# The causal mask of the last score block: added on VectorE in the maximum instead of on TensorE

## The chip, the core and the metric

The kernel runs on one core of a Trainium2 chip. The metric is the time of one execution on the device, in microseconds (us). The engines that matter here are PE (TensorE, matrix products), PEld (its weight loads), DVE (VectorE), ACT (ScalarE), POOL (GpSimd) and SP (it issues most transfers). They run side by side and wait for one another by semaphores. PE and DVE meet in PSUM: PE writes scores into a bank, DVE reads them out.

## What is computed

The program is a stack of four layers on a tensor of 4 x 512 x 256: an attention with rotary positions and biases, a mixture of experts with eight experts, a second attention, and a gated mixture of experts. Each is followed by a normalisation and added to its input. Only the two attentions are touched. Both have 16 heads of 16 numbers and a causal mask:

```python
scores = jnp.einsum('bshd,bthd->bhst', q, k) / jnp.sqrt(HEAD_DIM)
causal = jnp.tril(jnp.ones((S, S), dtype=bool))[None, None]
scores = jnp.where(causal, scores, -jnp.inf)
probs = jax.nn.softmax(scores, axis=-1)
out = jnp.einsum('bhst,bthd->bshd', probs, v)
```

The softmax needs the largest allowed score of every row, for every head and each of the 512 rows of a sequence.

## The kernel before

One function, `attention_phase`, is run twice: at about 31 to 235 us of the span for the first attention and at about 559 to 775 us for the second. Its work is cut into `STEPS` = 16 steps, one for each of 4 sequences and 4 groups of `HPG` = 4 heads. A step T has `MAXES` = 11 slots s. In slot s PE makes one **maxima unit** of step T (`max_unit`, L966): scores of 128 query rows against the keys that they may see. It then makes one **probability unit** of the step before (`prob_unit`, L985), which ACT turns into exponentials (L906) and POOL masks (L540). Fills of other work (projections, transposes, outputs) stand between them at fixed slots.

The maxima units of a step are, by `max_work`: k = 0 to 3, one head each, 512 keys wide; k = 4 to 7, 384 wide; k = 8 and 9, two heads each, 256 wide; and **k = 10, the four-head unit**: the first 128 rows of all four heads against their first 128 keys, four blocks of 128 columns in one PSUM bank. They rotate over `A_BANKS` = 3 banks (named `shared` in the first attention, `a_ps_a` in the second). PE waits on `a_free` before it takes a bank, DVE on `a_full` before it reads one.

DVE finds the maxima in `unit_max`. For k below 10 it uses a fused operation (L1274, L1280) that adds the mask `mask_f` to the scores, writes the sum to `masked_s`, and keeps the negated maximum, which a short second instruction (READ_ACCUMULATOR) puts into `nmax`. For k = 10 the mask is not added by DVE: PE adds it into the bank with one more product, the identity `identb` times `mask_q` in bfloat16 (L970), and one TENSOR_REDUCE (L1285) gives the four maxima.

After unit 10 DVE splits the maxima of the step into two parts (`split_max`, L1295 and L1297, tile `nm`). PE transposes `nm` in `less` (L996), which stands in slot 2 of the next step in the first attention and, in the second, between products with the values in slot 1. ACT copies the result next to the queries (L761), and only then can the probability units of that step start. PE does this work in its own fixed order, so where `nm` is late, everything behind L996 on PE is late. DVE too has a fixed order: between its maxima stand evacuations of projections (L1234, L1254), the division of outputs (L1305, L1307) and the normalisations.

The order of each engine is written out in the loops over T and s; nothing is scheduled at run time.

Of the kernel before, what the change touches and what calls it, by code (L numbers as in the profile page):

```python
# [13 lines left out]
ALU = mybir.AluOpType  # L14
ACT = mybir.ActivationFunctionType
AX_X = mybir.AxisListType.X

P = 128
BATCH, SEQ, D = 4, 512, 256
# [7 lines left out]
HPG = HEADS // GROUPS  # L27
STEPS = BATCH * GROUPS
EPS = 1e-5
NEG = -1e38  # L30
# [139 lines left out]
STACKS = 3  # L170
# [4 lines left out]
LEAD = 96  # L175
# [17 lines left out]
def max_work(k):  # L193

    if k < 4:
        return [(k, 3, 0)]
    if k < 8:
        return [(k - 4, 2, 0)]
    if k < 10:
        return [(2 * (k - 8), 1, 0), (2 * (k - 8) + 1, 1, 2 * P)]  # L200
    return [(h, 0, h * P) for h in range(HPG)]
# [95 lines left out]
def attention_phase(nc, keep, w, layer, route, w1=None, w2=None, early=None, stacks=None, wide=None, first=None):  # L297
# [15 lines left out]
    with ExitStack() as ctx:  # L313
# [639 lines left out]
        def _(pe):  # L953
            def max_unit(t, k):

                n = t * MAXES + k
                ps = ps_a[n % A_BANKS]
                need(pe, a_free, n - A_BANKS + 1)
                if n < HPG:
                    pe.wait_ge(first_keys[n], 16)  # L960
                work = max_work(k)
                i, wd = work[0][1], (work[0][1] + 1) * P
                together = min(len(work), PER_TILE)
                for n in range(0, len(work), together):
                    h, _, at = work[n]
                    last = nc.tensor.matmul(ps[:, at:at + together * wd], q_st[t % STACKS][0:LEAD, h // PER_TILE, i * P:wd],  # L966
                                            k_st[t % STACKS][0:LEAD, h:h + together, 0:wd], start=(n == 0), stop=(k < 10),
                                            skip_group_check=True)
                if k == 10:
                    last = nc.tensor.matmul(ps[:, :], identb[:, :], mask_q[:, :].unsqueeze(1).to_broadcast([P, HPG, P]),  # L970
                                            start=False, stop=True, skip_group_check=True)
                last.then_inc(a_full, 1)

            def prob_unit(t, k):
# [241 lines left out]
        def _(dve):  # L1216
# [48 lines left out]
            def unit_max(t, k):  # L1265
                n = t * MAXES + k
                ps = ps_a[n % A_BANKS]
                dve.wait_ge(a_full, n + 1)
                if k < 8:
                    i, h = 3 - k // 4, k % 4  # L1270
                    wd = (i + 1) * P
                    if n > 1:
                        dve.wait_ge(a_free, n - 1)
                    nc.vector.tensor_tensor_reduce(masked_s[n % 2][:, 0:wd], ps[:, 0:wd], mask_f[:, SEQ - wd:SEQ], -1.0,  # L1274
                                                   -NEG, ALU.add, ALU.min, nmax[:, t % 2, i, h:h + 1]).then_inc(a_free, 1)
                    return
                if k < 10:
                    dve.wait_ge(a_free, n - 1)
                    for h, i, at in max_work(k):
                        last = nc.vector.tensor_tensor_reduce(masked_s[n % 2][:, at:at + 2 * P], ps[:, at:at + 2 * P],  # L1280
                                                              mask_f[:, SEQ - 2 * P:SEQ], -1.0, -NEG, ALU.add, ALU.min,
                                                              nmax[:, t % 2, i, h:h + 1])
                    last.then_inc(a_free, 1)
                    return
                nc.vector.tensor_reduce(nmax[:, t % 2, 0, :], ps[:, :].rearrange("p (h n) -> p h n", h=HPG), AX_X, ALU.max,  # L1285
                                        negate=True).then_inc(a_free, 1)

            def split_max(t):

# [1366 lines left out]
```

## Time and profile before

| | us |
|---|---|
| median of 3 runs | 990.11 |
| lowest and highest | 988.4, 990.35 |
| the profiled execution | 992.42 |
| its span, first to last instruction | 990.7 |
| busy in the span: PE | 916.7 |
| PEld | 718.8 |
| DVE | 605.8 |
| ACT | 492.0 |
| POOL | 439.3 |

The profiled execution lies 1.7 us outside its span and 2.3 us above the median of the runs. PE is busy for 93% of the span. Its busy time counts matmuls from start to modelled end, and neighbours overlap, so what one more matmul costs is read from the distance of the ends, not from its duration. The same holds for DVE: the next operation often starts before the one before has ended.

### The profile page before, as it was taken

The page shows a single profiled execution, that of the slowest core. Times are in us where ns is not written, and L with a number is a line of the kernel's source. Part 1 is how long each engine was busy: PE and PEld are TensorE (multiplying, and loading weights), DVE is VectorE, ACT ScalarE, POOL GpSimd, SP SyncE. Part 2 cuts the span into 40 slices and gives each one's busy share as a digit, 9 for nine tenths or more (in the row PEclk, how much of TensorE's full clock was granted, in tenths as well). Part 3 has the DMA queues.
Part 4 walks back from the last instruction along what each step waited for, and adds up shares of the span by engine and source line. Part 5 has one row for each costly group of instructions (what it writes and reads, how often), then busy time and mean ns, then how long its engine had stood idle before and what let it go on. Part 6 is the DMA issues. An engine that isn't in the chain of part 4 may idle for free. (4 is left out here: it accounts for less than half of the span.)

```text
span 990.7 us, 16978 instructions
## 1 busy us (share of the span) xinstructions
PE 916.7 (93%) x5620; PEld 718.8 (73%) x5620; DVE 605.8 (61%) x1961; ACT 492.0 (50%) x887; POOL 439.3 (44%) x416
## 2 busy tenths in 40 slices
PE   6899999999899999999992889999999779999997
PEld 4566766765688999999982556576756468888886
DVE  5677798988763444444444687887786246363535
ACT  6366666665333344443336265767676344343332
POOL 4453444436742333232236455455263455535333
PEclk9799999999999999999995898999999699999999
DMA  5443222201225322323104663534320010212201
GB/s 186 159 177 112 97 75 97 75 20 41 102 99 190 136 86 96 138 103 130 69 21 139 222 223 96 177 113 159 123 75 23 1 54 1 97 45 74 81 39 42
DMA packets 51964, 98.88 MB, mean 100 GB/s; under 512 B 7579, under 2 KB 23835, under 8 KB 51766
## 3 DMA queue, kind: packets, MB, share of 16 engines
q1 hardware_dynamic: 48822, 89.62, 26.3%
q0 software_dynamic: 3072, 8.39, 2.7%
q8 instruction: 36, 0.59, 0.2%
q14 instruction: 34, 0.28, 0.1%
HBM read 61.63 MB, written 36.36 MB: 99 GB/s over the span
## 5 line engine op out<-in xcount | busy, mean ns | idle before, releaser
L906 ACT ACTIVATE a_probs<-a_ps_b 128x512 f32<-128x512 f32 x240 | 142.0, 602 | 65.3 <-PE a_ps_b L985 62.4
L540 POOL TENSOR_SCALAR_AFFINE_SELECT a_probs<-a_probs 128x512 f32<-128x512 f32 x128 | 80.8, 649 | 136.2 <-ACT a_probs L906 136.1
L2074 PE MATMUL exp_ps_o<-w_both,exp_h_hi 128*128 128x512 f32 x320 | 115.7, 402 | 0.7 <-POOL w_both L1960 0.7
L985 PE MATMUL a_ps_b<-a_q_st,a_k_st 104*128 104x256 f32 (+3 forms) x384 | 104.7, 335 | 2.9 <-ACT a_probs L906 2.1
L1987 ACT ACTIVATE exp_h_hi<-shared 128x320 fp32r<-128x320 f32 x128 | 54.3, 440 | 86.0 <-PE shared L2057 86.0
L1274 DVE CUSTOM_DVE_ANT_0 a_masked_s<-shared,a_mask_f 128x512 f32<-128x512 f32 (+1 forms) x128 | 76.6, 620 | 31.8 <-PE shared L966 29.5
L2220 POOL TENSOR_TENSOR dense_h_lo<-dense_mixed,dense_h_hi 128x512 fp32r<-128x512 f32 x40 | 53.2, 1330 | 96.6 <-ACT dense_h_hi L2285 96.6
L1274 DVE CUSTOM_DVE_ANT_0 a_masked_s<-a_ps_a,a_mask_f 128x512 f32<-128x512 f32 (+1 forms) x128 | 76.5, 621 | 31.6 <-PE a_ps_a L966 29.0
L966 PE MATMUL a_ps_a<-a_k_st,a_q_st 96*128 96x512 f32 (+1 forms) x192 | 89.7, 483 | 5.8 <-DVE a_nmax L1274 5.0
L2031 DVE SCALAR_TENSOR_TENSOR exp_h_lo<-shared,exp_h_hi 128x320 fp32r<-128x320 f32 x128 | 61.4, 490 | 54.6 <-ACT exp_h_hi L1987 53.8
L966 PE MATMUL shared<-a_k_st,a_q_st 96*128 96x512 f32 (+1 forms) x176 | 90.0, 519 | 3.1 <-DMA a_k_st<-scratch 3.1
L1006 PE MATMUL a_ps_pv<-a_probs,a_v 128*32 128x512 f32 (+3 forms) x1024 | 89.9, 461 | 3.2 <-POOL a_probs L540 3.2
L2076 PE MATMUL exp_ps_o<-w_both,exp_h_lo 128*128 128x256 f32 x320 | 89.7, 280 | 0.0
L985 PEld LDWEIGHTS a_ps_b<-a_q_st,a_k_st 104*128 104x128 f32 x384 | 71.8, 193 | 24.4 <-ACT a_probs L906 14.6
L2057 PE MATMUL shared<-exp_x_t_hi,w_hi 128*128 128x320 f32 x256 | 79.2, 309 | 0.3 <-DVEq L2024 0.3
L2057 PE MATMUL shared<-exp_x_t_hi,w_lo 128*128 128x320 f32 x256 | 79.1, 309 | 0.0
L2057 PE MATMUL shared<-exp_x_t_lo,w_hi 128*128 128x320 f32 x256 | 79.1, 309 | 0.0
L1960 POOL TENSOR_TENSOR w_both<-w_raw,w_both 128x2048 fp32r<-128x2048 f32 x8 | 37.1, 4640 | 86.6 <-ACT w_both L1977 86.6
L2074 PEld LDWEIGHTS exp_ps_o<-w_both,exp_h_hi 128*128 128x128 f32 x320 | 60.1, 188 | 13.9 <-issue 1.0
L906 ACT ACTIVATE a_probs<-shared 128x512 f32<-128x512 f32 x80 | 48.3, 604 | 43.2 <-PE shared L985 42.7
L2515 DVE TENSOR_TENSOR dense_product<-dense_gated,dense_ps_u 128x512 f32<-128x512 f32 x40 | 27.5, 687 | 66.9 <-PE dense_ps_u L2305 59.8
L2285 ACT CAST dense_h_hi<-dense_mixed 128x512 fp32r<-128x512 f32 x40 | 24.8, 620 | 81.7 <-DVE dense_mixed L2534 51.7
(326 smaller groups left out, 2244.8 us busy)
## 6 DMA issues: line engine op xcount, KB each, us to landing
w_raw<-in_m_w SPq DMA_DIRECT2D x16, 1024.0 KB, 5.4
scratch<-a_hi SPq DMA_DIRECT2D x24, 512.0 KB, 3.0
dense_mix_rows<-mix_rows SPq DMA_DIRECT2D x9, 768.0 KB, 6.4
scratch<-a_lo SPq DMA_DIRECT2D x24, 256.0 KB, 3.2
a_q_st<-scratch SPq DMA_DIRECT2D x64, 96.0 KB, 2.2
a_k_st<-scratch SPq DMA_DIRECT2D x64, 96.0 KB, 2.3
exp_rows<-dispatched SPq DMA_DIRECT2D x9, 640.0 KB, 3.9
dispatched<-kept_sub SPq DMA_DIRECT2D x9, 512.0 KB, 2.8
```

The source lines that it names most:

```text
L540: nc.gpsimd.affine_select(out=blocks, in_=blocks, compare_op=ALU.is_ge, fill=0.0, base=0, pattern=[[0, HPG], [1, P]], channel_multiplier=- ...
L906: nc.scalar.activation(probs[:, k, :], ps_b[k % B_BANKS][:, :], ACT.Exp, scale=scale).then_inc(exps, 1)
L966: last = nc.tensor.matmul(ps[:, at:at + together * wd], q_st[t % STACKS][0:LEAD, h // PER_TILE, i * P:wd], k_st[t % STACKS][0:LEAD, h:h + ...
L985: last = nc.tensor.matmul(ps[:, at:at + wd], k_st[t % STACKS][0:TAIL, h, j * P:(j + 1) * P], q_st[t % STACKS][0:TAIL, h // PER_TILE, j * P ...
L1006: last = nc.tensor.matmul(ps_pv[h * VW:(h + 1) * VW, at:SEQ], v[:, b % 2, j, g * HPG + h, :], rhs, start=(j == 0), stop=(j == 2), skip_gro ...
L1274: nc.vector.tensor_tensor_reduce(masked_s[n % 2][:, 0:wd], ps[:, 0:wd], mask_f[:, SEQ - wd:SEQ], -1.0, -NEG, ALU.add, ALU.min, nmax[:, t % ...
L1987: nc.scalar.activation(h[0][:, f, half * HALF:(half + 1) * HALF], ps_u[n % U_BANKS][:, 0:HALF], ACT.Relu).then_inc(u_hi, 1)
L2031: nc.vector.scalar_tensor_tensor(h[1][:, f, cols], ps_u[n % U_BANKS][:, 0:HALF], 0.0, h[0][:, f, cols].bitcast(F32), ALU.max, ALU.subtract ...
L2057: last = nc.tensor.matmul(ps_u[(2 * f + half) % U_BANKS][:, 0:HALF], (w1["hi"], w1["lo"])[i][:, c, f * P:(f + 1) * P], x_t[j][:, c * CAP + ...
L2074: nc.tensor.matmul(bank[:, :], h[0][:, f, rows_at], w2["both"][:, f, :, :].rearrange("p k d -> p (k d)"), start=(f == 0), stop=False, skip ...
L2076: last = nc.tensor.matmul(bank[:, 0:D], h[1][:, f, rows_at], w2["hi"][:, f, :], start=False, stop=(f == FC - 1), skip_group_check=True)
L2220: nc.gpsimd.tensor_tensor(h[1][:, (m - 1) % H_BUFS, :], mixed[(m - 1) % 2][:, :], h[0][:, (m - 1) % H_BUFS, :].bitcast(F32), ALU.subtract) ...
```

## The change

In both attentions PE no longer adds the mask to the four-head unit: L970 goes, and the score product's `stop` is now always true. DVE takes unit 10 as it takes the others: four fused operations of 128 columns, each with its READ_ACCUMULATOR, in place of one TENSOR_REDUCE over 512 columns. The last of the eight instructions releases the bank. Before them DVE also waits on `a_free` for the unit two before, since `masked_s` has two buffers.

```diff
--- before.py
+++ after.py
@@ -964,11 +964,8 @@
                 for n in range(0, len(work), together):
                     h, _, at = work[n]
                     last = nc.tensor.matmul(ps[:, at:at + together * wd], q_st[t % STACKS][0:LEAD, h // PER_TILE, i * P:wd],
-                                            k_st[t % STACKS][0:LEAD, h:h + together, 0:wd], start=(n == 0), stop=(k < 10),
+                                            k_st[t % STACKS][0:LEAD, h:h + together, 0:wd], start=(n == 0), stop=True,
                                             skip_group_check=True)
-                if k == 10:
-                    last = nc.tensor.matmul(ps[:, :], identb[:, :], mask_q[:, :].unsqueeze(1).to_broadcast([P, HPG, P]),
-                                            start=False, stop=True, skip_group_check=True)
                 last.then_inc(a_full, 1)
 
             def prob_unit(t, k):
@@ -1274,16 +1271,13 @@
                     nc.vector.tensor_tensor_reduce(masked_s[n % 2][:, 0:wd], ps[:, 0:wd], mask_f[:, SEQ - wd:SEQ], -1.0,
                                                    -NEG, ALU.add, ALU.min, nmax[:, t % 2, i, h:h + 1]).then_inc(a_free, 1)
                     return
-                if k < 10:
-                    dve.wait_ge(a_free, n - 1)
-                    for h, i, at in max_work(k):
-                        last = nc.vector.tensor_tensor_reduce(masked_s[n % 2][:, at:at + 2 * P], ps[:, at:at + 2 * P],
-                                                              mask_f[:, SEQ - 2 * P:SEQ], -1.0, -NEG, ALU.add, ALU.min,
-                                                              nmax[:, t % 2, i, h:h + 1])
-                    last.then_inc(a_free, 1)
-                    return
-                nc.vector.tensor_reduce(nmax[:, t % 2, 0, :], ps[:, :].rearrange("p (h n) -> p h n", h=HPG), AX_X, ALU.max,
-                                        negate=True).then_inc(a_free, 1)
+                dve.wait_ge(a_free, n - 1)
+                for h, i, at in max_work(k):
+                    wd = (i + 1) * P
+                    last = nc.vector.tensor_tensor_reduce(masked_s[n % 2][:, at:at + wd], ps[:, at:at + wd],
+                                                          mask_f[:, SEQ - wd:SEQ], -1.0, -NEG, ALU.add, ALU.min,
+                                                          nmax[:, t % 2, i, h:h + 1])
+                last.then_inc(a_free, 1)
 
             def split_max(t):
```

On PE, first attention, from the scores of unit 10 of step 2 (L966 into the bank `shared2`) to the transposes of its `nm` (L996) in step 3; L985 are probability units of step 1. Before:

```order
L966 MATMUL shared2<-a0_k_st2,a0_q_st2 128x512 [waits a0_a_free]
L970 MATMUL shared2<-kept_mask_q,kept_identb 128x512
L985 MATMUL a0_ps_b1<-a0_q_st1,a0_k_st1 128x384 [waits a0_exps]
L985 MATMUL a0_ps_b1<-a0_q_st1,a0_k_st1 128x128
L966 MATMUL shared0<-a0_k_st0,a0_q_st0 128x512 [waits a0_a_free,a0_stacked0]
L985 MATMUL shared3<-a0_q_st1,a0_k_st1 128x256 [waits a0_exps]
L985 MATMUL shared3<-a0_q_st1,a0_k_st1 128x256
L966 MATMUL shared1<-a0_k_st0,a0_q_st0 128x512 [waits a0_a_free]
L985 MATMUL a0_ps_b1<-a0_q_st1,a0_k_st1 128x256 [waits a0_exps]
L985 MATMUL a0_ps_b1<-a0_q_st1,a0_k_st1 128x256
L966 MATMUL shared2<-a0_k_st0,a0_q_st0 128x512 [waits a0_a_free]
L996 MATMUL a0_ps_m1<-a0_identr,a0_nm 104x128 [waits a0_nm_ready,a0_m_free1]
```

With the change (line numbers behind L970 are 3 lower):

```order
L966 MATMUL shared2<-a0_k_st2,a0_q_st2 128x512 [waits a0_a_free]
L982 MATMUL a0_ps_b1<-a0_q_st1,a0_k_st1 128x384 [waits a0_exps]
L982 MATMUL a0_ps_b1<-a0_q_st1,a0_k_st1 128x128
L966 MATMUL shared0<-a0_k_st0,a0_q_st0 128x512 [waits a0_a_free,a0_stacked0]
L982 MATMUL shared3<-a0_q_st1,a0_k_st1 128x256 [waits a0_exps]
L982 MATMUL shared3<-a0_q_st1,a0_k_st1 128x256
L966 MATMUL shared1<-a0_k_st0,a0_q_st0 128x512 [waits a0_a_free]
L982 MATMUL a0_ps_b1<-a0_q_st1,a0_k_st1 128x256 [waits a0_exps]
L982 MATMUL a0_ps_b1<-a0_q_st1,a0_k_st1 128x256
L966 MATMUL shared2<-a0_k_st0,a0_q_st0 128x512 [waits a0_a_free]
L993 MATMUL a0_ps_m1<-a0_identr,a0_nm 104x128 [waits a0_nm_ready,a0_m_free1]
```

Only the product L970 has gone; the order around it is the same.

On DVE, the end of the same step: the output division of step 0, unit 10 of step 2, the split, and the first maximum of step 3. Before:

```order
L1305 RECIPROCAL a0_rsum<-a0_ps_m0 128x16 [waits a0_m_full0]
L1307 TENSOR_TENSOR kept_sub<-a0_ps_m0,a0_rsum 128x4x64 [waits a0_rsum_ready]
L1285 TENSOR_REDUCE a0_nmax<-shared2 128x4 [waits a0_a_full]
L1295 CAST a0_nm<-a0_nmax 128x4x4 [waits a0_m_full1,a0_a_free]
L1297 TENSOR_TENSOR a0_nm<-a0_nmax,a0_nm 128x4x4 [waits a0_nm_hi]
L1274 ISA a0_masked_s1,a0_nmax<-shared0,a0_mask_f 128x512 [waits a0_a_free,a0_a_full]
```

With the change (ISA is the fused operation; `a0_nmax 128x1` behind it is its READ_ACCUMULATOR):

```order
L1299 RECIPROCAL a0_rsum<-a0_ps_m0 128x16 [waits a0_m_full0]
L1301 TENSOR_TENSOR kept_sub<-a0_ps_m0,a0_rsum 128x4x64 [waits a0_rsum_ready]
L1277 ISA a0_masked_s0,a0_nmax<-shared2,a0_mask_f 128x128 [waits a0_a_free,a0_a_full]
L1277 ISA a0_nmax 128x1
L1277 ISA a0_masked_s0,a0_nmax<-shared2,a0_mask_f 128x128
L1277 ISA a0_nmax 128x1
...
L1289 CAST a0_nm<-a0_nmax 128x4x4 [waits a0_m_full1,a0_a_free]
L1291 TENSOR_TENSOR a0_nm<-a0_nmax,a0_nm 128x4x4 [waits a0_nm_hi]
L1271 ISA a0_masked_s1,a0_nmax<-shared0,a0_mask_f 128x512 [waits a0_a_free,a0_a_full]
```

Eight instructions stand where one stood, ahead of the split; nothing has changed places.

## Rows read from the trace of the kernel before

**Rows 1.** Stretches, the two attentions: us, busy PE, PEld, DVE, ACT, POOL, PEclk, DMA share, GB/s.

```profile
25.00:235.00 210.00, 201.31 (x1306) 139.21 (x1308) 167.88 (x610) 125.25 (x238) 95.16 (x113) 0.97 0.29 98
555.00:775.00 220.00, 207.96 (x1294) 136.43 (x1292) 166.53 (x603) 141.91 (x262) 114.67 (x131) 0.98 0.39 127
```

**Rows 2.** Groups by line and shape, DVE: xcount | busy us, mean ns | idle us before.

```profile
L1274 DVE CUSTOM_DVE_ANT_0 a_masked_s<-shared,a_mask_f 128x384 f32<-128x384 f32 x64 | 34.2, 554 | 13.1 <-PE shared L966 12.2 <-DVE a_part_q L1234 0.5
...
L1280 DVE CUSTOM_DVE_ANT_0 a_masked_s<-shared,a_mask_f 128x256 f32<-128x256 f32 x64 | 24.3, 419 | 6.6 <-PE shared L966 5.3 <-PE shared L970 0.5 <-DVE a_prior L1400 0.3
...
L1285 DVE TENSOR_REDUCE a_nmax<-shared 128x4 f32<-128x512 f32 x16 | 10.9, 683 | 1.0 <-PE shared L970 1.0
```

**Rows 3.** Timeline of DVE, step 8, first attention: start us, duration us, engine, line.

```profile
136.05 0.41 DVE L1280 CUSTOM_DVE_ANT_0 a_masked_s<-shared,a_mask_f 128x256 f32<-128x256 f32 x1
...
136.39 0.41 DVE L1280 CUSTOM_DVE_ANT_0 a_masked_s<-shared,a_mask_f 128x256 f32<-128x256 f32 x1
```

**Rows 4.** The line of the mask product: count, min/median/max ns, first and last start.

```profile
L970 PE MATMUL shared<-kept_mask_q,kept_identb x16: 390/391/650, 39.3 to 228.9; 128*128 128x512 bf16 x16
...
L970 PE MATMUL a_ps_a<-kept_mask_q,kept_identb x16: 390/390/587, 569.5 to 762.0; 128*128 128x512 bf16 x16
```

**Rows 5.** Timeline of PE, end of step 8, first attention.

```profile
134.83 0.50 PE L966 MATMUL shared<-a_k_st,a_q_st 96*128 96x512 f32 x1
135.16 0.41 PE L985 MATMUL a_ps_b<-a_q_st,a_k_st 104*128 104x384 f32 x2
...
136.45 0.44 PE L966 MATMUL shared<-a_k_st,a_q_st 96*128 96x512 f32 x1
136.74 0.39 PE L970 MATMUL shared<-kept_mask_q,kept_identb 128*128 128x512 bf16 x1
136.78 0.59 PE L985 MATMUL a_ps_b<-a_q_st,a_k_st 104*128 104x384 f32 x2
```

**Rows 6.** Timeline, start of step 8, first attention.

```profile
127.20 0.68 DVE L1285 TENSOR_REDUCE a_nmax<-shared 128x4 f32<-128x512 f32 x1
...
127.92 0.17 DVE L1295 CAST a_nm<-a_nmax 128x16 fp32r<-128x16 f32 x1
...
128.13 0.18 DVE L1297 TENSOR_TENSOR a_nm<-a_nmax,a_nm 128x16 fp32r<-128x16 f32 x1
...
128.38 2.07 POOL L540 TENSOR_SCALAR_AFFINE_SELECT a_probs<-a_probs 128x512 f32<-128x512 f32 x3
...
128.59 0.50 PE L996 MATMUL a_ps_m<-a_identr,a_nm 128*104 128x128 f32 x4
```

**Rows 7.** Timeline, the split and its reader: first and last of 32 pairs.

```profile
40.90 0.18 DVE L1297 TENSOR_TENSOR a_nm<-a_nmax,a_nm 128x16 fp32r<-128x16 f32 x1
...
42.88 0.50 PE L996 MATMUL a_ps_m<-a_identr,a_nm 128*104 128x128 f32 x4
...
765.20 0.18 DVE L1297 TENSOR_TENSOR a_nm<-a_nmax,a_nm 128x16 fp32r<-128x16 f32 x1
...
765.52 0.56 PE L996 MATMUL a_ps_m<-a_identr,a_nm 128*104 128x128 f32 x4 [0.70 <-DVE a_nm L1297]
```

**Rows 8.** Timeline of PE, end of step 5, second attention.

```profile
638.72 1.12 PE L1070 MATMUL a_ps_m<-a_y_t,a_w_qk 128*128 128x512 f32 x2 [0.22 <-DVE a_lo L1254]
```

**Rows 9.** Timeline, start of step 7, first attention.

```profile
112.62 1.23 POOL L540 TENSOR_SCALAR_AFFINE_SELECT a_probs<-a_probs 128x512 f32<-128x512 f32 x2 [2.46 <-ACT a_probs L906]
...
113.00 0.29 DVE L1295 CAST a_nm<-a_nmax 128x16 fp32r<-128x16 f32 x1
...
113.33 0.55 DVE L1297 TENSOR_TENSOR a_nm<-a_nmax,a_nm 128x16 fp32r<-128x16 f32 x1
```

**Rows 10.** All calls of the split: count, min/median/max ns.

```profile
L1297 DVE TENSOR_TENSOR a_nm<-a_nmax,a_nm x32: 175/178/566, 40.9 to 765.2; 128x16 fp32r<-128x16 f32 x32
```

**Rows 11.** Stretches, steps 2 and 3 of the second attention; columns as in rows 1.

```profile
593.80:597.20 3.40, 2.11 (x12) 1.35 (x10) 3.40 (x13) 1.47 (x3) 0.89 (x2) 1.00 0.00 0
597.20:600.60 3.40, 3.11 (x14) 1.86 (x14) 3.30 (x19) 1.52 (x3) 1.26 (x3) 0.51 0.00 0
```

## The prediction

> **What bounds the kernel now.** I read the busy time by stretch first: the change touches only the two attentions, and there PE is busy for 201 of 210 us and 208 of 220 us, at the full granted clock (0.97 and 0.98 of it, 2.4 GHz, in the mean), while DVE is busy for 168 and 167 us [rows 1]. So PE is the engine to relieve and DVE the one with room. A mean of 80% is not yet room at the place of the change, though. For that I went to the timelines at the end of a step, and asked two things: is PE held up by the mask product, and how soon after DVE's work on unit 10 does PE need its result? The result travels from unit 10 by the cast and the subtraction (L1295, L1297) to the transposes L996, behind which all of PE's order is queued: the products with the values, the maxima and the probability units of the step.
>
> **What is removed on PE.** The product L970 takes 0.39 us at full clock [rows 4], but its neighbours overlap with it. By ends: the score product of unit 10 ends at 136.45 + 0.44 = 136.89, L970 at 136.74 + 0.39 = 137.13, the next probability unit at 136.78 + 0.59 = 137.37. Two units earlier, where no mask product stands between, the same two ends are 135.33 and 135.57. The distance is 0.48 with it and 0.24 without: **L970 costs 0.23 us** (0.233 in unrounded records; 30 of the 32 pairs agree within 0.002) [rows 5]. In step 0 of each attention it ran partly at the lower clock, 0.65 and 0.59 us long [rows 4]; there I take 0.45 and 0.39.
>
> **What is added on DVE.** The trace has the fused operation at 384 and 256 columns, 554 and 419 ns, so 135 ns for each 128 columns [rows 2]. Back to back, the one of 256 starts every 0.34 us, its READ_ACCUMULATOR included [rows 3]. For 128 columns that gives a distance of 0.34 - 0.135 = 0.21 us, and the last read ends 0.08 after the last distance: 4 x 0.21 + 0.08 = 0.93 us to the release, against 0.68 for the reduction [rows 2]. **The split comes 0.25 us later.** Bounds from the nearest rows: not under 4 x 0.135 + 0.08 = 0.62 (columns alone, a gain of 0.06), not over four distances of the wider form, 4 x 0.34 + 0.08 = 1.44 (a loss of 0.76). I take 0.25, because the distance is a straight line over the two widths. The added wait on `a_free` asks for a unit that DVE itself finished two units ago, and L1280 has it too and starts back to back; nothing. The mask no longer passes through PE's bank, so `a_full` comes 0.23 us earlier, but DVE mostly arrives late at unit 10 because of the output division before it, and uses it only in the two steps 0 and in step 14 of the first attention. The eight instructions in place of one delay the first maxima of the next step too; with three banks PE needs those 0.4 us or more after their release nearly everywhere, and where not, L996 is the tighter wait.
>
> **What is left of it, step by step.** Call margin the time from the end of L1297 to the start of L996, less 0.15, which is the shortest such distance (a pair where PE waits). The first pair has 42.88 - 41.08 - 0.15 = 1.65, the last 765.52 - 765.38 - 0.15 = 0 [rows 7]. Over the 32 pairs, in the first attention: 1.66, 0.19, 0, 0.69, 0.59, 0.38, 0.69, 0.14, 0, 0.38, 0.81, 0.14, 0.03, 0.16, 1.77, 0; in the second: 1.16, 0, 1.09, 1.89, 0.93, 1.42, 0, 1.33, 1.15, 1.42, 1.89, 1.33, 0.04, 0.93, 1.89, 0. PE comes 0.23 earlier and the split 0.25 later, so a margin under 0.48 is used up. A step gives -0.23 plus what 0.48 exceeds its margin by:
> - steps 0: -0.45 and -0.39, together -0.84;
> - 13 steps with a margin over 0.48: 13 x -0.233 = -3.03;
> - margin 0.38, twice: -0.27;
> - six steps with 0.19 to 0.03: +0.06, +0.11, +0.11, +0.09, +0.22, +0.20, together +0.79;
> - six with margin 0, where PE already waits: 6 x 0.25 = +1.48;
> - steps 5 and 9 of the second attention: PE waits right behind L970 for DVE's evacuation L1254, whose time comes from before L970 [rows 8]: 0;
> - step 2 of the second attention, where DVE works without a pause and PE waits for banks: +0.25.
>
> Sum: -1.6 us.
>
> **A second term, POOL.** L1297 takes 175 ns in some steps and up to 566 in others [rows 10]; 14 of 32 are over 0.4 us. In the timeline each long one ends with a POOL mask operation (L540): the pair that starts at 112.62 is over at 113.85, the cast ends at 113.29 and L1297 at 113.88 [rows 9]; the cast was held by its first half and the split by its second. L540 follows exponentials that PE feeds after L970, so it comes 0.23 earlier while the cast comes 0.25 later. I moved the two against each other in every step. In step 7 the cast ran free from 127.92 and the next L540 began at 128.38 [rows 6]; now the cast starts at 128.17 and POOL at 128.15: it is held, or just escapes. Taking a held operation to end 0.03 after POOL's, the steps that matter change by -0.27 (steps 1 and 8, and 1 of the second attention), -0.32 (13), +0.12 (2), +0.26, +0.24, +0.38, +0.27 (7, 11, 12, 15), +0.11 and +0.23 (12, 15 of the second): **+0.5 in all**. The Trainium skill (SBUF — State Buffer, the section on the port pair that VectorE and GpSimd share) gives the cause: a VectorE instruction with two SBUF inputs, or in a two-port mode, and a GpSimd instruction exclude each other for the whole instruction, and PSUM sources are free of it. The trace agrees: the fused operations, with one input in PSUM, keep their duration.
>
> Result: -1.6 + 0.5 = **-1.1 us**, on the profiled execution 992.42 - 1.1 = 991.3, on the median (2.3 lower) 990.11 - 1.1 = **989.0 us**.
>
> **Rivals.**
> 1. *The small operations don't overlap* (slower). If a fused operation of 128 columns held DVE for its duration, 0.42 - 0.135 = 0.285 us, unit 10 would take 4 x 0.285 + 0.08 = 1.22, and the split would be 0.54 late. The same list gives +3.2 us, with POOL +4.8: about 994. It decides from a lateness of 0.36, where the list passes zero. Against it: the wider ones overlap by 0.08 [rows 3]. The Trainium skill (VectorE: DVE Perf Modes, the section on the TRN2 errata) speaks for this direction: small operations pay a fixed term each, so it wants 512 or more elements, and its table has 120 cycles plus the columns from PSUM. An estimate by that page: 248 cycles or 0.26 us each, 0.43 late, and the list gives +1.2 us, 991.3.
> 2. *PE had the time of L970 to spare.* If the exponentials or a bank fixed the next unit, removing it gives nothing while the split is still 0.25 later: +2.5 us, 992.6. Against it: the ends in rows 5, where the clock of the products runs through.
> 3. *The split isn't in the way* (faster). If DVE makes up the lateness, every step but 5 and 9 keeps its gain: 28 x -0.233 - 0.84 = -7.4, 982.7; if the four operations cost as much as the one, -5.0, 985.1. Against it: PE waits in six pairs already.
> 4. *The clock.* At 597.2 the granted level fell from full to half (0.51), after PE had been busy for only 2.11 of 3.40 us [rows 11]; that is where DVE holds PE up. 0.5 us more of such waiting, or a shift of the work against it, can add or remove a piece of similar length at half clock, up to 1.7 us: 990.7 or 987.3.
>
> That the change does not do what it says is ruled out by the order of both engines.
>
> **Chances.** Forecast 0.50, its own range 987.3 to 990.3, since each POOL slot is 0.3 us either way; rival 1 0.13; rival 2 0.07; rival 3 0.12, mostly at 985; rival 4 0.18, half on each side. Within 0.2% (2.0 us, about what a measurement of this kernel can tell from no change) lies most of the forecast and half of rival 4. Faster by more: rival 3, half of rival 4 and the low tail of the forecast, 0.30. Slower by more: rivals 1 and 2 and a little of the rest, 0.22. The range leaves out the ends of rivals 1 and 3: 985.5 to 993.5.
>
> **What would show it.** Right: fused operations of 128 columns about 285 ns long and 0.21 apart; unit 10 to release 0.93; no L970, and PE's two ends 0.24 apart there; PE's waits for L1297 more than before, and in more steps; attentions shorter by about 0.2 and 1.0 us. Wrong: a distance of 0.28 or more (rival 1), the next unit starting no earlier (2), no new waits at L996 (3), other half-clock stretches (4).

## The result, and the profile after

The changed kernel takes 992.57 us in the median of 20 runs, the kernel before 989.55 us in 20 runs beside it: ratio **1.0038, 95% interval 1.0025 to 1.0051**. The forecast was 989.0 us, faster by 1.1. The time lies in the range, but on the other side: the change makes the kernel about 3 us slower. The profiled execution of after took 992.51 us, its span is 990.8 us. The one of before was 2.9 us above its kernel's median, so this pair of traces differs by only 0.1 us in all. What can be compared in it are pieces: one step, one wait, one operation. In all the experiments below one run had another state of the clock: a run of `att0_only` took 1290.06 us at a granted clock of 0.65, and it counts in the median there but in no ratio.

Stretches of after, the columns as in [rows 1]:

```profile
25.00:235.00 210.00, 197.54 (x1266) 136.15 (x1264) 169.26 (x714) 123.15 (x235) 91.55 (x110) 0.97 0.30 97
555.00:775.00 220.00, 207.04 (x1283) 134.86 (x1281) 173.15 (x719) 138.57 (x257) 112.03 (x129) 0.98 0.42 135
```

In the first attention PE is now busy for 197.5 of 210 us instead of 201.3 [rows 1]. Of the 40 products fewer (1266 instead of 1306) only 16 are L970; the other 24 are missing because the stretch now ends earlier in the program. PE does less and gets less far.

The groups of DVE, by line and shape, as in [rows 2] (L1271 was L1274, L1277 was L1280; L1285 is gone):

```profile
L1271 DVE CUSTOM_DVE_ANT_0 a_masked_s<-shared,a_mask_f 128x384 f32<-128x384 f32 x64 | 34.2, 554 | 13.0 <-PE shared L966 12.4 <-DVE a_part_q L1231 0.5
...
L1277 DVE CUSTOM_DVE_ANT_0 a_masked_s<-shared,a_mask_f 128x256 f32<-128x256 f32 x64 | 24.3, 419 | 6.6 <-PE shared L966 5.3 <-DVE a_part_k L1231 0.8 <-DVE a_prior L1394 0.3
...
L1277 DVE CUSTOM_DVE_ANT_0 a_masked_s<-shared,a_mask_f 128x128 f32<-128x128 f32 x64 | 14.7, 285 | 0.5 <-PE shared L966 0.5
```

The form of 128 columns takes 285 ns. How four of them follow one another, and what comes behind, stands in the timeline of after at the end of step 6 of the first attention (start us, duration us, engine, line):

```profile
113.00 0.28 DVE L1277 CUSTOM_DVE_ANT_0 a_masked_s<-shared,a_mask_f 128x128 f32<-128x128 f32 x1
...
113.20 0.28 DVE L1277 CUSTOM_DVE_ANT_0 a_masked_s<-shared,a_mask_f 128x128 f32<-128x128 f32 x1
113.25 1.22 POOL L540 TENSOR_SCALAR_AFFINE_SELECT a_probs<-a_probs 128x512 f32<-128x512 f32 x2 [2.38 <-ACT a_probs L906]
...
113.41 0.28 DVE L1277 CUSTOM_DVE_ANT_0 a_masked_s<-shared,a_mask_f 128x128 f32<-128x128 f32 x1
...
113.83 0.08 DVE L1277 DVE_READ_ACCUMULATOR2_ANT a_nmax<- 128x1 f32 x1
113.95 0.56 DVE L1289 CAST a_nm<-a_nmax 128x16 fp32r<-128x16 f32 x1
...
114.54 0.18 DVE L1291 TENSOR_TENSOR a_nm<-a_nmax,a_nm 128x16 fp32r<-128x16 f32 x1
```

The starts are 0.21 us apart, and from 113.00 to the end of the last read at 113.91 it is 0.91 us. Then the cast is held to 114.51, until POOL's pair has ended (113.25 + 1.22 = 114.47). In [rows 9] both the cast and L1297 had been held in this place.

The end of a step on PE, as in [rows 5] (the unit of step 8 of the first attention with its neighbour, in after):

```profile
137.74 0.45 PE L966 MATMUL shared<-a_k_st,a_q_st 96*128 96x512 f32 x1
138.02 0.40 PE L982 MATMUL a_ps_b<-a_q_st,a_k_st 104*128 104x384 f32 x2
```

The ends are 138.19 and 138.42: 0.23 apart, where it was 0.48. And the waits of PE for the split, in the list of waits (waiting engine, tile, line <- releaser: us, times, longest). Before:

```profile
PE a_ps_m L996 <- DVE a_nm L1297: 2.6, 3, 1.4
```

After:

```profile
PE a_ps_m L993 <- DVE a_nm L1291: 6.6, 8, 2.4
```

4.0 us more, in five more steps. 2.4 us of it lies in the first attention (1.9 us became 4.3), 1.6 us in the second (0.7 became 2.3).

A useful measure of what a wait costs in the end is the length of a step: from the start of its first maxima product (L966) to that of the next. Steps of one program without a stretch at half clock repeat to 0.05 us from trace to trace in all places of the first attention but one (see `twin` and `again`). First attention, in us, where * marks a step with a stretch at half clock; steps 0 and 1 are left out, because such stretches lie in them in some traces and not in others (step 1 is 10.85 us in before, 12.41 in after and 12.37 in `pe_only`); "last" is from the scores of unit 10 of step 15 to the transposes of its split (L996 or its counterpart):

| step | 2 | 3 | 4 | 5 | 6 | 7 | 8 | 9 | 10 | 11 | 12 | 13 | 14 | 15 | last |
|---|---|---|---|---|---|---|---|---|---|---|---|---|---|---|---|
| before | 10.74 | 12.67 | 11.44 | 13.82 | 12.04 | 13.86 | 11.46 | 14.08 | 12.52 | 13.86 | 11.63 | 13.82 | 13.43 | 11.37 | 3.54 |
| after | 10.68 | 13.06 | 11.49 | 13.66 | 12.02 | 13.63 | 12.34 | 14.21 | 12.56 | 13.62 | 12.32 | 13.97 | 13.45 | 11.37 | 4.31 |
| `pe_only` | 10.53 | 12.47 | 11.47 | 13.66 | 11.97 | 13.62 | 11.63 | 13.95 | 12.49 | 13.62 | 11.60 | 13.98 | 13.44 | 11.39 | 3.54 |
| `dve_only` | 10.85 | 13.28 | 11.45 | 13.82 | 12.02 | 13.85 | 12.12 | 14.36 | 12.56 | 13.86 | 12.27 | 13.83 | * | 11.47 | 4.31 |
| `yield0_after` | 10.52 | 12.41 | 11.49 | 13.69 | 12.01 | 13.61 | 11.92 | 13.68 | 12.54 | 13.62 | 11.88 | 13.84 | 13.45 | 11.38 | 3.83 |

Second attention, steps 4 to 15, which hold no such stretch: before 149.3 us, after 148.4, `pe_only` 148.4, `dve_only` 149.2.

### The profile page after: what moved, and what is told of

The parts are those of the page before. It is cut to its first block and busy times, and to the rows that moved or that the text cites. A ratio compares the mean times of both kernels' runs of the same rounds, so it can differ in the third digit from the quotient of the medians.

```text
span 990.8 us, 17170 instructions
## 1 busy us (share of the span) xinstructions
PE 913.7 (92%) x5588; PEld 717.5 (72%) x5588; DVE 613.9 (62%) x2185; ACT 490.3 (49%) x887; POOL 438.2 (44%) x416
## 5 line engine op out<-in xcount | busy, mean ns | idle before, releaser
L982 PE MATMUL a_ps_b<-a_q_st,a_k_st 104*128 104x256 f32 (+3 forms) x384 | 101.4, 328 | 2.5 <-ACT a_probs L906 1.6
L1271 DVE CUSTOM_DVE_ANT_0 a_masked_s<-shared,a_mask_f 128x512 f32<-128x512 f32 (+1 forms) x128 | 76.4, 620 | 31.1 <-PE shared L966 29.1
L966 PE MATMUL a_ps_a<-a_k_st,a_q_st 96*128 96x512 f32 (+1 forms) x192 | 89.0, 480 | 6.4 <-DVE a_nmax L1271 5.1
L966 PE MATMUL shared<-a_k_st,a_q_st 96*128 96x512 f32 (+1 forms) x176 | 91.5, 528 | 3.5 <-DMA a_k_st<-scratch 3.2
L1271 DVE CUSTOM_DVE_ANT_0 a_masked_s<-a_ps_a,a_mask_f 128x512 f32<-128x512 f32 (+1 forms) x128 | 75.9, 620 | 26.1 <-PE a_ps_a L966 24.3
```

Source lines behind the costliest of these rows:

```text
L982: last = nc.tensor.matmul(ps[:, at:at + wd], k_st[t % STACKS][0:TAIL, h, j * P:(j + 1) * P], q_st[t % STACKS][0:TAIL, h // PER_TILE, j * P ...
```

## The experiments

The theory before the first of them: the split comes late, and what that costs outweighs what PE gains. Rivals: PE gains nothing to begin with, or the difference is the clock's. Each kernel is compared with the kernel before on the same chip. The ratios are those on record with their intervals; they are not quotients of the two medians, from which they differ by up to 0.3%. The first four kernels here ran beside 989.52 us of before, the next four on another chip beside 1003.59, the last three beside 989.00.

**`again`: the changed kernel once more, unaltered.**

> The changed kernel once more, on the chip of the three runs that follow, so that they have a common reference and a second trace. Theory M (the cost lies between unit 10 and L996: margins and POOL slots, and the two steps 0 save nothing, since PE waits there for an evacuation by ACT) gives about -0.3 us against the kernel before by my list of steps. Theory C (the loss is outside the attention steps: other stretches at half clock, the exchange between the attention and the experts) gives +3 us as measured, with attention steps that sum to about what M says.

994.03 us, 1.0047 (1.0030 to 1.0065). The result repeats, and theory M with its -0.3 us falls. The steps in its trace agree with those of after to 0.03 us in 13 of 14 (steps 2 to 15); step 13 is 14.44 instead of 13.97. The rows of the split before it show why. In after:

```profile
194.31 0.18 DVE L1291 TENSOR_TENSOR a_nm<-a_nmax,a_nm 128x16 fp32r<-128x16 f32 x1
194.31 0.68 POOL L540 TENSOR_SCALAR_AFFINE_SELECT a_probs<-a_probs 128x512 f32<-128x512 f32 x1
```

In `again`:

```profile
194.40 0.64 DVE L1291 TENSOR_TENSOR a_nm<-a_nmax,a_nm 128x16 fp32r<-128x16 f32 x1
194.38 0.63 POOL L540 TENSOR_SCALAR_AFFINE_SELECT a_probs<-a_probs 128x512 f32<-128x512 f32 x1
```

It is the same program. In after POOL's record starts 0.003 us ahead of DVE's, and DVE runs free; in `again` it starts 0.017 us ahead, and L1291 lasts until POOL has ended, 0.47 us longer. The whole step is longer by that much. So where the two engines meet, a hundredth of a microsecond decides over half a microsecond.

**`pe_only`: PE's part alone.** L970 goes, DVE keeps its one reduction.

```diff
-                if k == 10:
-                    last = nc.tensor.matmul(ps[:, :], identb[:, :], mask_q[:, :].unsqueeze(1).to_broadcast([P, HPG, P]),
-                                            start=False, stop=True, skip_group_check=True)
```

> PE's part alone: the mask product L970 is left out, and DVE's single reduction stays, so the mask of unit 10 is added nowhere and its maxima run over all 128 keys of the block. Theory M: every step but four gains 0.23 us less what POOL slots take, -4.4 us, about -2.2 in each attention. Rival 2 of the prediction (PE had that time to spare): within 0.5 us of no change. Theory C: the gain is there in the steps of the trace but not in the time.

990.21 us, 1.0001 (0.9985 to 1.0016). Theory M's -4.4 us falls, and rival 2's time holds; the 7 us that the mask products cost by the distance of the ends are not there. The steps show where part of them goes. Steps 4, 6, 10, 12 and 14 are as long as before, within 0.07; step 2 and the odd ones 3, 5, 7, 9 and 11 are 0.13 to 0.24 us shorter, steps 8 and 13 even 0.17 and 0.16 longer. Step 4 ends so on PE and ACT in before:

```profile
84.94 0.50 PE L985 MATMUL shared<-a_q_st,a_k_st 104*128 104x384 f32 x2
85.27 0.45 PE L966 MATMUL shared<-a_k_st,a_q_st 96*128 96x512 f32 x1
85.56 0.39 PE L970 MATMUL shared<-kept_mask_q,kept_identb 128*128 128x512 bf16 x1
85.60 0.59 PE L985 MATMUL a_ps_b<-a_q_st,a_k_st 104*128 104x384 f32 x2
86.09 1.10 PE L1070 MATMUL a_ps_m<-a_y_t,early_qk 128*128 128x512 f32 x2
...
85.24 0.71 ACT L730 ACTIVATE a_y_t<-a_ps_m,early_rms_w 128x512 f32<-128x512 f32 x1
```

and so in `pe_only`:

```profile
84.77 0.51 PE L982 MATMUL shared<-a_q_st,a_k_st 104*128 104x384 f32 x2
85.11 0.45 PE L966 MATMUL shared<-a_k_st,a_q_st 96*128 96x512 f32 x1
85.39 0.40 PE L982 MATMUL a_ps_b<-a_q_st,a_k_st 104*128 104x384 f32 x2
85.92 1.10 PE L1067 MATMUL a_ps_m<-a_y_t,early_qk 128*128 128x512 f32 x2
...
85.07 0.71 ACT L730 ACTIVATE a_y_t<-a_ps_m,early_rms_w 128x512 f32<-128x512 f32 x1
```

From the scores of unit 10 to the fill (L1070, now L1067) it is 0.82 us with L970 and 0.81 without. The probability unit between them ends at 86.19 with L970, after the fill has begun, and at 85.79 without, 0.13 before it. In both the fill starts 0.14 us after ACT's evacuation into `a_y_t` (L730) has ended: 85.95 and 86.09, 85.78 and 85.92. L970 stood in time that PE would have waited for ACT. The same 0.14 us behind L730 stands at the end of steps 0 and 8. In step 0 the wait shows by name, in the timeline of after:

```profile
38.72 2.04 PE L1067 MATMUL a_ps_m<-a_y_t,early_qk 128*128 128x512 f32 x2 [0.44 <-ACT a_y_t L730]
```

At the end of steps 6 and 10 the fill is L1077 and reads `a_o_t`. In `pe_only` its weight load waits there for ACT's evacuation into that tile, 0.17 us each time, which it doesn't in before; this is from the waits of PEld between 60 and 230 us:

```profile
PEld a_ps_m L1077 <- ACT a_o_t L768: 0.3, 2, 0.2
```

For steps 8, 12, 13 and 14 the lengths are not traced to a wait here.

**`dve_only`: DVE's part alone.** L970 stays, and DVE adds the mask once more on top of it, in four fused operations (the maxima are the same).

> DVE's part alone: the mask product stays on PE and DVE adds the mask a second time with its four fused operations. Theory M: the split is 0.25 us later, PE is not earlier: +2.3 us (+1.3 and +1.0), paid in the steps where PE already waits or nearly does, and in POOL slots. If lateness of the split were harmless: 0. If it costs more than the list says (each late step drags POOL and ACT too): +4 or more.

993.88 us, 1.0045 (1.0020 to 1.0070): all of the loss of the changed kernel, without its PE part, and about the +4 that was named for lateness that drags POOL along. The table has it in few places: steps 3, 8 and 12 are 0.61, 0.66 and 0.64 us longer, step 9 0.28, the last pair 0.77; six of the others within 0.02. In the second attention steps 4 to 15 together lose nothing (149.2 for 149.3). In the traces the first attention is 3.2 us longer, without step 14, where +1.3 was expected, and the second 0.1, where +1.0 was expected.

What makes a lateness of 0.25 us into 0.6 to 0.8 is POOL, as `yield0_after` below confirms. The last pair shows it best. In before, first attention, step 15:

```profile
230.82 0.68 DVE L1285 TENSOR_REDUCE a_nmax<-shared 128x4 f32<-128x512 f32 x1
231.54 0.17 DVE L1295 CAST a_nm<-a_nmax 128x16 fp32r<-128x16 f32 x1
231.75 0.18 DVE L1297 TENSOR_TENSOR a_nm<-a_nmax,a_nm 128x16 fp32r<-128x16 f32 x1
...
232.07 0.92 PE L996 MATMUL a_ps_m<-a_identr,a_nm 128*104 128x128 f32 x4 [1.40 <-DVE a_nm L1297]
...
232.03 2.17 POOL L540 TENSOR_SCALAR_AFFINE_SELECT a_probs<-a_probs 128x512 f32<-128x512 f32 x3
```

and in after, where everything up to here is 2.1 us later:

```profile
232.92 0.29 DVE L1277 CUSTOM_DVE_ANT_0 a_masked_s<-shared,a_mask_f 128x128 f32<-128x128 f32 x1
...
233.88 0.18 DVE L1289 CAST a_nm<-a_nmax 128x16 fp32r<-128x16 f32 x1
234.09 0.65 DVE L1291 TENSOR_TENSOR a_nm<-a_nmax,a_nm 128x16 fp32r<-128x16 f32 x1
...
234.08 1.21 POOL L540 TENSOR_SCALAR_AFFINE_SELECT a_probs<-a_probs 128x512 f32<-128x512 f32 x2
...
234.89 0.93 PE L993 MATMUL a_ps_m<-a_identr,a_nm 128*104 128x128 f32 x4 [2.40 <-DVE a_nm L1291]
```

Before, the split was over at 231.93, 0.10 us before POOL began. Now it starts at 234.09, 0.01 us after POOL, and lasts 0.65 instead of 0.18. PE's wait grows by 1.0 us, the way from unit 10 to the transposes from 3.54 to 4.31.

**`yield_after`: the changed kernel, with POOL out of the split's way.** The mask operation of the second quarter of a step waits until the split of the next step is done, so it can't hold it.

```diff
                 pool.wait_ge(exps, t * PROBS + (4, 8, 8, 10)[n])
+                if n == 1:
+                    pool.wait_ge(nm_ready, min(t + 2, STEPS))
```

> The changed kernel, where POOL waits with the masks of blocks 1 and 3 of a step (causal, n = 1) until DVE has done the split of the next step, so that no mask operation can hold the cast or L1291. Theory M with POOL slots: the split no longer takes up to 0.63 us, and the time falls by 2.5 us against the changed kernel, -2.9 against the kernel before at best; less by what the later masks hold up the products with the values. If the POOL slots are not what costs: no change against the changed kernel, or slower by the later masks.

992.07 us, 1.0018 (0.9995 to 1.0041). This is below `again` by 0.3%, but the intervals overlap. The wait has a price of its own. In the second attention PE's products with the values wait for POOL's masks for 5.1 us, where it is 1.4 in before and 1.3 in after; in the first one their weight loads wait for them for 5.4 us, where it is 1.6 in before.

**`att0_only` and `att1_only`: the whole change in one attention.** The conditions of both parts get `and rope` or `and not rope`; `rope` is true in the first attention.

> The whole change (no L970, four fused operations) in the first attention alone. Theory M, as the runs so far have corrected it: here lateness of the split is paid (steps 3, 8, 12) and PE's gain is lost in the even steps, where the fill behind L970 waits for ACT. The step sum of the trace rises by 1.5 to 2 us without the clock. Time: +2.5 to +4.5 with its share of half clock. If the loss sat in the second attention: within 1 us of no change.

1006.89 us, 1.0055 (1.0030 to 1.0080).

> The whole change in the second attention alone. Theory M: the steps sum to 0.7 us less (lateness is absorbed there by later waits, PE gains 0.15 to 0.23 in most steps), so -0.7 us and at most 1 us of clock either way. Theory C in its strong form (any removal of PE work puts more of the run at half clock): mean clock 0.002 to 0.004 lower than before and +1 us or more.

1002.20 us, 0.9999 (0.9978 to 1.0019). The loss comes from the first attention. In the second one the PE gain seen in the steps, 0.9 us, is below what a comparison of this size can tell; against it stands +0.23 in step 2.

**`yield0_after` and `yield0_before`: POOL waits in the first attention only**, with and without the change.

```diff
+                if n == 1 and rope:
+                    pool.wait_ge(nm_ready, min(t + 2, STEPS))
```

> The changed kernel with POOL yielding to the split in the first attention only. Yielding in both took 2 us off the changed kernel in the median, while its trace shows a step sum 4.7 us lower in the first attention and new waits for late masks in the second. Theory M with POOL slots: 3 to 4 us faster than the changed kernel, at or 1 us under the kernel before. If that drop was luck of the clock: no more than 1 us faster than the changed kernel.

1000.84 us, 0.9999 (0.9980 to 1.0019).

> The kernel before, with POOL yielding to the split in the first attention only. Theory M: here the split is early enough in most steps, so only 0.8 us is to be had: -0.5 to -1.5 us. If the yielding itself saves time whatever the split does: -3 to -4, as for the changed kernel.

1002.15 us, 1.0000 (0.9978 to 1.0022). With the wait the changed kernel is no slower than before, and its interval lies below that of `att0_only`. The step table says the same: in `yield0_after` step 3 is 0.65 us shorter than in after, step 8 0.42, step 9 0.53, step 12 0.44, the last pair 0.48. So the loss goes when POOL can no longer catch the split. What remains in step 12 (0.25 over before) and the last pair (0.29) is the lateness itself; in step 8 it is 0.46, of which `pe_only` has 0.17 without any lateness. Without the change the wait shows no gain in the whole; the -0.5 to -1.5 expected are less than this comparison can tell, and in the trace of `yield0_before` steps 3 and 9 are 0.48 and 0.26 us shorter than in before.

**`late0`: the lateness made larger.** In the first attention of the changed kernel four more fused operations precede those of unit 10, into tiles that nobody reads.

```diff
+                if k == 10 and rope:
+                    for h, i, at in max_work(k):
+                        nc.vector.tensor_tensor_reduce(extra_s[:, at:at + P], ps[:, at:at + P], mask_f[:, SEQ - P:SEQ], -1.0,
+                                                       -NEG, ALU.add, ALU.min, extra_m[:, h:h + 1])
```

> The changed kernel, and in the first attention DVE takes four more fused operations of 128 columns ahead of the four of unit 10, into tiles that nobody reads; the split comes 4 x 0.21 = 0.84 us later still. Theory (the loss is lateness of the split in the first attention): of the 16 steps only 0 and 14 have more than 0.84 of margin left, four have 0.1 to 0.3, ten have none; 14 x 0.84 - 0.9 = +10.9 us over the changed kernel in steps 1 to 15 and the tail, ratio to before about 1.014, and nothing in the second attention. Rival (the loss of the change comes from the lower granted clock that PE's idle time brings, and lateness itself is mostly made up within the step, as in the second attention): under +4 us over the changed kernel, ratio under 1.008.

1010.22 us, 1.0183 (1.0145 to 1.0221). Over the changed kernel that is 17.6 us by the medians and 14 by the ratios (about 4 to each side, from four runs), where the theory had 10.9 and the rival less than 4. The rival falls; the theory's 1.014 lies just under the interval, but its mechanism isn't confirmed. Steps 2 to 15 are 13.6 us longer than in after, and 9.4 of that lie in the four steps that hold a stretch at half clock (3, 8, 13 and 14). The ten others are 4.2 us longer together, where 10 x 0.84 would be 8.4; the last pair adds 1.2. In `twin` below one such stretch makes a step 1.64 us longer. By an estimate from that number four of them are about 6.6 us, and the lateness itself about 8 of the 14.8, where the theory had 10.9. So lateness in the first attention is expensive, less so than the margins say, and half-clock stretches come on top. A second path is in it, in the waits of the first attention:

```profile
PE shared L967 <- DVE a_nmax L1282: 4.2, 6, 1.2
PE a_ps_m L994 <- DVE a_nm L1296: 2.5, 4, 0.8
```

(L1282 holds all maxima of k = 8 to 10, L994 is the transposes.) Here PE waits less for the split than in after (4.3), and 4.2 us for banks, which these operations release 0.84 us later; in after that is 0.4 us, once. So part of the loss comes by the bank, which the expectation had left out, and this run alone doesn't give a price for the split.

**`yield0_pe_only`: PE's part without DVE's, and POOL out of the way.** This asks whether the POOL slots are what ate PE's gain.

> The kernel before without the mask product on PE in both attentions (the mask of unit 10 is then added nowhere, and the one reduction of DVE is kept), and with POOL's mask operation of slot 1 of the first attention waiting for the split. Theory (PE's gain is eaten by what PE waits for one fill later, ACT's and DVE's evacuations, and by the clock): even steps of the first attention as long as before, the second attention 0.7 to 1 us shorter, ratio 0.997 to 1.000. Rival (the gain of the mask product was taken back by the POOL slots, which hit the split without it just as well): with POOL out of the way the 0.233 us show in nearly every step, -7 us, ratio 0.993.

988.90 us, 0.9994 (0.9969 to 1.0018). They aren't: steps 4, 6, 10, 12 keep their lengths within 0.07 (11.47, 11.97, 12.49, 11.60), and the whole is no faster than before. Over all but step 14, which holds a stretch at half clock, steps 2 to 15 of the first attention are 1.7 us shorter than before, and steps 4 to 15 of the second 1.0, as the theory had it.

**`twin`: the kernel before once more.**

> The kernel before once more under another name, for what two traces of one program differ by. Theory (part of the differences between single traces is where the stretches at half clock fall): steps that hold no such stretch agree within 0.05 us, the others differ by up to 3 us, ratio 1.000 with an interval of 0.0015 to each side. Rival (traces of one program agree throughout, so every difference between traces of before and after is the change's): all steps within 0.05 us.

991.23 us, 1.0011 (0.9992 to 1.0031). Of the 16 steps of the first attention 14 agree to 0.02 us between the two traces, and the rival falls. In the second attention step 4 differs by 0.11 although no stretch at half clock lies in it. In the first, step 0 is 8.52 instead of 9.15 and step 14 15.07 instead of 13.43. The same stretch in both traces shows why for step 14; columns as in [rows 1]. Before:

```profile
204.60:208.00 3.40, 3.40 (x34) 2.45 (x37) 3.13 (x9) 1.65 (x3) 1.73 (x3) 1.00 0.24 63
```

`twin`:

```profile
204.60:208.00 3.40, 3.40 (x24) 1.09 (x27) 1.36 (x6) 0.58 (x1) 0.25 (x1) 0.52 0.37 98
```

The same program at the same place: at the lower level of the granted clock (0.52, which is 1.2 GHz) PE finishes 24 products instead of 34, and the step is 1.64 us longer. Whether such a stretch comes can differ from one execution to the next.

## Why the prediction was wrong

Two steps of it failed. The gain of L970 was put at 0.233 us in 28 of 32 steps, where the traces have about 1.8 us in all of the 7.4 that this makes with the two steps 0. And the price of the late split in the first attention was put at about 1.35 us by the margins and 0.4 by the POOL slots, where the trace of `dve_only` has 3.2 in all.

**DVE's part was sized right.** 285 ns for an operation, 0.21 us apart, 0.91 to the release (0.93 in the prediction). Rival 1 fell with that: the small operations overlap like the wide ones. The Trainium skill (VectorE: DVE Perf Modes, the section on the TRN2 errata) gives, by an estimate from its 120 cycles plus columns, 0.26 us each; that is nearer to the duration of one than to the distance of two, and here the distance decides.

**PE's part was sized right at the spot and wrong one fill further.** The ends lie 0.23 apart in after, as forecast. But the step "13 steps free, -3.03" took that for a shorter step. In `pe_only` the steps 2 to 15 of the first attention together are 0.9 us shorter, where 14 x 0.233 = 3.3 would be the price by the ends; steps 4 to 15 of the second 0.9, where the prediction has 10 x 0.233 = 2.3. Step 0, with -0.45 and -0.39 in the prediction, has the wait for `a_y_t` instead: in the second attention it is 11.29 us in before and in after. Rival 2 asked the right question, whether PE had the time of L970 to spare, and I dismissed it with the ends in [rows 5]: they run through for one probability unit, and the fill that waits for ACT stands behind that. It was given a chance of 0.07 and a time of 992.6. That 992.57 was measured is luck: some of the gain does arrive, and the lateness costs more than rival 2 had.

**The lateness costs more, in few places.** The margin list has +0.79 and +1.48 for the twelve tight steps and +0.5 for POOL. In the first attention `dve_only` has steps 3, 8, 12 and the last pair at +0.6 to +0.8 each, 2.7 together, most others at nothing. The POOL term named the right pairs (2, 7, 11 and 15, whose price falls in steps 3, 8, 12 and the last stretch) with +0.12 to +0.27 each. The steps have 0.24 to 0.29 more for each than the term and the margin list together: 0.61 in step 3 against 0.25 + 0.12, 0.66 in step 8 against 0.11 + 0.26. Pair 12, listed at +0.38, shows nothing in `dve_only` (step 13, +0.01) and +0.62 in `again`; the gains of -0.27 and -0.32 don't show. The reason is in the timelines of the last pair and of pair 12 in after and `again`: 0.1 us, at pair 12 even 0.01, in the start of POOL or DVE decides between 0 and 0.47. I moved the two by fixed amounts to hundredths of a microsecond [rows 6, 9], while PE's and ACT's waits move them too.

**The second attention came nearly as forecast**, -0.9 in steps 4 to 15 and +0.23 in step 2, against "about 1.0" shorter in all. Part of that is luck: step 0 gains nothing where -0.39 stood, and the last pair, with +0.25 and +0.23 for POOL in the prediction, costs nothing in the end. POOL does hold the split there, and the transposes come 0.69 us later after unit 10 than before; but the products with the values, which in before wait for POOL's masks at this place, start 4.81 us after unit 10 in after and 4.80 in before. The first attention didn't come so: "0.2 shorter" against +1.6 in steps 2 to 15 and +0.8 in the last pair. So the miss is the first attention's. The pieces seen add up to +1.7 us.

**The rest is probably the clock, and that is argued, not shown.** Over 33 runs of before the time falls with the mean granted clock by 4.5 us for each 0.01 (correlation -0.86). The mean clock was 0.9670 in them and 0.9620 in the runs of `again` on the same chip, which by that slope is +2.2 us. Together that is 3.9, where 4.5 (medians) to 4.7 (ratio) was measured for `again`, and 3.0 to 3.8 for the first 20 runs. `pe_only` has 0.9628, +1.9 by the slope, and 0.9 + 0.9 us of shorter steps, and its time is that of before: there what PE gained was given back at the lower level. The drop isn't tied to the late split. `pe_only` and `yield0_pe_only` (0.9627 for 0.9674), which have no late split, lose nearly as much clock as `again`, and so do `att1_only` (0.9595 for 0.9635) and `yield0_after` (0.9585 for 0.9635). The kernels that keep L970 in one attention or both lose less, `dve_only` 0.0031, `twin` 0.0019, `att0_only` 0.0015 and `yield0_before` 0.0013, each uncertain by about 0.001 to 0.002. That points to the missing products, but `yield_after`, which lacks them too, has 0.9666 and doesn't fit. Nor does the slope fit everywhere: for `att1_only` and `yield0_after` it and the steps give about +1.2 us, and none was measured, with 2 us to each side. A place where the lower clock shows is the tail of the first attention, up to the first expert product: 73.3 us in before, 73.5 in `twin`, 79.0 in after, 78.8 in `again`. Of the 5.7 only 0.8 is in the last pair. In before:

```profile
265.40:268.50 3.10, 3.10 (x24) 2.62 (x23) 0.65 (x6) 0.55 (x2) 2.62 (x3) 0.88 0.26 87
268.50:278.70 10.20, 10.20 (x77) 10.10 (x77) 8.49 (x50) 4.27 (x12) 6.47 (x7) 1.00 0.26 91
```

In after:

```profile
265.40:268.50 3.10, 2.05 (x10) 1.22 (x10) 3.03 (x10) 0.72 (x2) 1.52 (x3) 1.00 0.01 3
268.50:278.70 10.20, 10.20 (x46) 9.73 (x45) 3.72 (x31) 5.16 (x13) 7.68 (x8) 0.50 0.29 100
```

PE was busy for 2.05 of 3.10 us, then had 10.2 us at the lower level, with 46 products in place of 77. Before, it had had the work to stay busy there. Both traces of the changed kernel show it and both of before don't; `dve_only` (77.7) and `late0` (79.6) lean to after, `pe_only` (75.4) stands between, and `yield_after` (72.7) and `yield0_pe_only` (74.0) lean to before. This isn't a loss of clock over the whole trace, though: before has stretches at half clock later, from 597.2 to 604.1 us among others, that after lacks, and the profiled execution of after has the higher mean, 0.964 against 0.963. Against it stands the second chip: there all four kernels have this tail at 82 to 83 us, `yield0_before` (81.9) as `att0_only` (81.8), and `att0_only` is still 0.55% slower than before. So the tail's stretch is not needed for the loss, and no experiment held the waits fixed and moved only the clock. How much of the 3 us is the clock's own, and what lowers it, stays open. Rival 4 had a piece of this size (1.7 us) with an even chance of either sign, where the mean clock of the changed kernel is lower.

## What to carry to other kernels

Taking work from the busiest engine gains only up to its next wait. Follow the order past the spot, until a product that waits for another engine (here, in five of the 16 steps of the first attention, the fill behind ACT's evacuation), and count the gain up to there; a chain of ends without a gap proves it for one unit alone. And where a short operation of DVE sits on the path close ahead of a POOL operation on SBUF, 0.25 us of delay can cost 0.7: look for the few places where the two meet, rather than multiply the delay by the number of steps. If such an operation can't be moved, let POOL wait for it; here that brought the time back to that of before and no further.

## What the hardware showed that I had not expected

Fused operations of 512, 384, 256 and 128 columns keep an overlap down to the shortest: 285 ns long, 0.21 us apart, the read of the accumulator included. L1291, an operation on 16 columns, took 645 ns where it started 0.01 us after a POOL operation, and 177 ns in the median; in two executions of the changed kernel the same call took 176 and 644 ns, with 0.003 and 0.017 us between the two starts. And two executions of one program, `twin` and before, have the same span to 0.1 us, with single steps that differ by 0.6 and 1.6 us, because the stretches at half clock fall on other places.
